# Second-layer scores of a two-layer transformer kernel as three float32r products, with keys and queries split one period ahead

## The reference, cut to what matters

```python
qkv = (h @ Wqkv.T).reshape(b, n, 3, H, HD)
q = _ln(qkv[:, :, 0].transpose(0, 2, 1, 3), qn_g, qn_b)
k = _ln(qkv[:, :, 1].transpose(0, 2, 1, 3), kn_g, kn_b)
v = qkv[:, :, 2].transpose(0, 2, 1, 3)
scores = jnp.einsum('bhnd,bhmd->bhnm', q, k) / jnp.sqrt(jnp.float32(HD))
attn = jax.nn.softmax(scores, axis=-1)
o = jnp.einsum('bhnm,bhmd->bhnd', attn, v)
x = x + o.transpose(0, 2, 1, 3).reshape(b, n, H * HD) @ Wout.T
```

## Time and profile before

| | us |
|---|---|
| runs of the kernel before | 390.44, 391.27, 391.53 (median 391.27) |
| the profiled execution, its own time | 391.85 |
| its span in the trace | 390.1 |
| granted TensorE clock, mean over the span | 0.959 of 2.4 GHz |

### The profile page before, as it was taken

How to read it: one execution, slowest core, us unless ns; L and a number is a source line. 1 busy time by engine, 2 the same in 40 slices (tenths; PEclk the granted TensorE clock), 3 DMA queues, 4 the chain that set the end, 5 groups by cost and what they waited for, 6 DMA issues and landing times.

```text
span 390.1 us, 8940 instructions
## 1 busy us (share of the span) xinstructions
PE 360.2 (92%) x3188; PEld 259.5 (67%) x3188; DVE 258.5 (66%) x608; ACT 267.2 (68%) x660; POOL 151.5 (39%) x158
## 2 busy tenths in 40 slices
PE   7998997769999999999999999999999886799994
PEld 7585676446666666676676676666665564589993
DVE  2856356658767767767767776776777448883425
ACT  3355646688887887887887999888896527347640
POOL 5500233465466466456556546556631011000000
PEclk9999999999999999999999999999999975569999
DMA  4900000002920000000000000000000000000001
GB/s 116 286 7 2 2 2 0 2 0 56 329 104 2 2 3 0 2 3 2 3 0 3 3 2 0 3 1 3 2 0 3 2 2 1 0 2 2 0 3 54
DMA packets 7520, 9.77 MB, mean 25 GB/s; under 512 B 379, under 2 KB 4278, under 8 KB 7478
## 3 DMA queue, kind: packets, MB, share of 16 engines
q1 hardware_dynamic: 5654, 7.11, 5.9%
q10 hardware_dynamic: 1824, 2.10, 1.9%
HBM read 8.68 MB, written 0.52 MB: 24 GB/s over the span
## 4 chain that ended last, share of the span: by engine, by line
PE 82%; DVE 8%; ACT 5%; issue 2%; POOL 1%; DVEq 0%; POOLq 0%; ACTq 0%
PE bank L1356 15%; PE pair L1307 8%; PE pair L1283 7%; PE bank L1307 7%; PE bank L1323 6%; PE bank L1085 6%; PE pair L1323 4%; PE bank L1334 4%; PE bank L1211 2%; PE bank L1501 2%; PE pair L1093 2%; PE pair L1343 2%; PE pair L1219 2%; PE pair L1425 1%; ACT probs L593 1%
## 5 line engine op out<-in xcount | busy, mean ns | idle before, releaser
L423 POOL TENSOR_TENSOR qk_rstd<-qk_ms,minus_half 128x8 f32<-128x8 f32 x32 | 52.5, 1641 | 99.0 <-DVE qk_ms L878 99.0
L1323 PEld LDWEIGHTS bank<-ident,probs 64*128 64x128 f32 x512 | 36.8, 139 | 46.6 <-issue 46.4
L1356 PE MATMUL bank<-probs_T,v_s 128*64 128x256 f32 x512 | 62.3, 385 | 0.6 <-DVE x_att L921 0.6
L890 DVE TENSOR_REDUCE negmax<-pair 128x1 f32<-128x512 f32 x64 | 43.8, 686 | 21.2 <-PE pair L1307 21.2
L602 ACT ACTIVATE probs_T<-bank 128x512 f32<-128x512 f32 x64 | 38.0, 594 | 24.2 <-PE pair L1323 24.0
L593 ACT ACTIVATE probs<-pair,negmax 128x512 f32<-128x512 f32 x64 | 43.9, 687 | 9.3 <-DVE negmax L890 8.3
L1323 PE MATMUL bank<-ident,probs 64*128 64x64 f32 x512 | 43.4, 225 | 2.2 <-DVE probs_T L898 1.3
L1356 PEld LDWEIGHTS bank<-probs_T,v_s 128*64 128x64 f32 x512 | 34.1, 136 | 16.5 <-issue 0.8
L1323 PE MATMUL pair<-ident,probs 64*128 64x64 f32 x512 | 45.1, 228 | 0.0
L898 DVE COPY probs_T<-pair 128x512 f32<-128x512 f32 x64 | 43.7, 683 | 1.1 <-PE pair L1323 1.1
L593 ACT ACTIVATE probs<-bank,negmax 128x512 f32<-128x512 f32 x64 | 43.6, 694 | 0.1
(11 more groups left out here) (252 smaller groups left out, 762.4 us busy)
## 6 DMA issues: line engine op xcount, KB each, us to landing
fc_raw<-in_L_cond_fc2s_dram SPq DMA_DIRECT2D x1, 2048.0 KB, 14.9
x_in<-in_x_dram ACTq DMA_DIRECT2D x1, 512.0 KB, 4.0
w<-in_L_cond_mlp_w_dram SPq DMA_DIRECT2D x2, 256.0 KB, 5.2
wout<-in_L_cond_Wout_dram SPq DMA_DIRECT2D x1, 512.0 KB
b_all<-in_L_cond_b2s_dram SPq DMA_DIRECT2D x1, 512.0 KB, 11.6
out_dram<-final SPq DMA_DIRECT2D x2, 256.0 KB, 2.3
film<-in_L_cond_film_w_dram SPq DMA_DIRECT2D x2, 128.0 KB, 4.3
wq<-in_L_cond_q_w_dram SPq DMA_DIRECT2D x1, 64.0 KB, 2.6
```

What stands on the lines that cost most here:

```text
L423: pool.tensor_tensor(qk_rstd[:, p % 2, :, :].rearrange("p c t -> p (c t)"), qk_ms[:, p % 2, :, :].rearrange("p c t -> p (c t)"), minus_hal ...
L890: dve.tensor_reduce(negmax[:, t % 2, h:h + 1], bank[2 * (t % 2) + h][:, :], AX, ALU.max, negate=True)\
L1323: last = pe.transpose(bank[(4, 6)[q]][:, n * HD:n * HD + HD], probs[rows, t % 2, n // NC, n % NC * P:n % NC * P + P], ident[rows, rows])
L1356: last = pe.matmul(bank[5][h * HD:h * HD + HD, 0:2 * P], v_s[:, m % 4, k, h * HD:h * HD + HD], probs_T[:, r % 2, h, k, :], start=(k == 0), ...
```

## The change

It takes the scores from one float32 product per head to three float32r products (high x high, high x low, low x high), each for both heads in turn. Keys and queries of a piece are now written by `piece_affine` to `kq_full` in float32; a new `keys_high` on VectorE rounds them to `kq_hi`, and a new `keys_low` on GpSimd subtracts to get `kq_lo`. All stages from `project` to `piece_affine` are moved one period ahead: projections at r+6, squares and sums at r+5, norms, turns and affines at r+4. So one more piece is made before the loop; there piece 3's norm goes from GpSimd to VectorE and piece 4's square to ScalarE. A smaller `tn_sq` makes room, for which one wait is added behind the loop.

```diff
-        keys_T = loop("keys_T", [P, 2, N])
-        queries_T = loop("queries_T", [P, 2, N])
+        kq_full = loop("kq_full", [P, 2, 2, 2 * P])
+        kq_hi = loop("kq_hi", [P, 2, 2, N], F32R)
+        kq_lo = loop("kq_lo", [P, 2, 2, N], F32R)
-        tn_sq = tokens("tn_sq", [P, TC, D])
+        tn_sq = tokens("tn_sq", [P, NC, D])
...
+            def keys_low(p):
+                m, half = p // 2, p % 2 * 2 * P
+                pool.wait_ge(kq_high, p + 1)
+                pool.tensor_tensor(kq_lo[:, m % 2, :, half:half + 2 * P], kq_full[:, p % 2, :, :],
+                                   kq_hi[:, m % 2, :, half:half + 2 * P].bitcast(F32), ALU.subtract)\
+                    .then_inc(kq_low, 1)
             norm_scale(2, 1, EPS1)
+            keys_low(0)
             piece_scale(2)
+            keys_low(1)
             piece_scale(3)
+            keys_low(2)
+            piece_scale(4)
             for r in range(HALVES):
                 spread_recip(r)
+                if r + 4 < HALVES:
+                    piece_norm(r + 4)
                 if r + 3 < HALVES:
-                    piece_norm(r + 3)
-                if r + 4 < HALVES:
-                    piece_square(r + 4)
-                    piece_scale(r + 4)
+                    keys_low(r + 3)
+                if r + 5 < HALVES:
+                    piece_square(r + 5)
+                    piece_scale(r + 5)
...
             def piece_affine(p):
-                m, half = p // 2, p % 2 * 2 * P
                 act.wait_ge(kqT_done, p + 1)
-                wait(act, scores_done, 8 * m - 8)
-                act.activation(keys_T[:, m % 2, half:half + 2 * P], turned(p)[:, 0:2 * P], ACT.Identity,
+                wait(act, kq_low, p - 1)
+                act.activation(kq_full[:, p % 2, 0, :], turned(p)[:, 0:2 * P], ACT.Identity,
...
             exponential(0, 0)
             exponential(0, 1)
+            piece_square(4)
             piece_raw(4)
             piece_affine(2)
             exponential(1, 0)
             exponential(1, 1)
+            piece_raw(5)
+            piece_affine(3)
             for r in range(HALVES):
...
-                if r + 3 < HALVES:
-                    piece_affine(r + 3)
-                if r + 5 < HALVES:
-                    piece_raw(r + 5)
+                if r + 4 < HALVES:
+                    piece_affine(r + 4)
+                if r + 6 < HALVES:
+                    piece_raw(r + 6)
...
+            act.wait_ge(tn_ss, NC)
...
+            def keys_high(p):
+                m, half = p // 2, p % 2 * 2 * P
+                dve.wait_ge(kq_affine, p + 1)
+                wait(dve, scores_done, 8 * m - 8)
+                dve.tensor_copy(kq_hi[:, m % 2, :, half:half + 2 * P], kq_full[:, p % 2, :, :]).then_inc(kq_high, 1)
             scaled(2, 1, xn)
+            keys_high(0)
             into_h(2)
             piece_norm(2)
+            keys_high(1)
             maximum(0, 0)
             maximum(0, 1)
             piece_ss(3)
             maximum(1, 0)
             maximum(1, 1)
+            piece_norm(3)
+            keys_high(2)
+            piece_ss(4)
             for r in range(HALVES):
...
                 if 2 * r + 2 < STEPS:
                     maximum(2 * r + 2, 0)
+                if r + 3 < HALVES:
+                    keys_high(r + 3)
                 copy_probs(2 * r)
...
-                if r + 4 < HALVES:
-                    piece_ss(r + 4)
+                if r + 5 < HALVES:
+                    piece_ss(r + 5)
...
             def turn_piece(p):
...
-                if p >= 3:
-                    pe.wait_ge(copied_act, 2 * (p - 3) + 2)
-                elif p == 2:
-                    pe.wait_ge(kq_affine, 1)
+                if p >= 4:
+                    pe.wait_ge(copied_act, 2 * (p - 4) + 2)
+                elif p >= 2:
+                    pe.wait_ge(kq_affine, (1, 3)[p - 2])
             def scores(t):
...
                 if c == 0:
-                    pe.wait_ge(kq_affine, 2 * i + 2)
-                for h in range(2):
-                    rows = slice(h * HD, h * HD + HD)
-                    pe.matmul(bank[2 * (t % 2) + h][:, :], queries_T[rows, i % 2, c * P:c * P + P],
-                              keys_T[rows, i % 2, :], start=True, stop=True).then_inc(scores_done, 1)
+                    pe.wait_ge(kq_high, 2 * i + 2)
+                for n, (queries, keys) in enumerate(((kq_hi, kq_hi), (kq_hi, kq_lo), (kq_lo, kq_hi))):
+                    if c == 0 and n == 1:
+                        pe.wait_ge(kq_low, 2 * i + 2)
+                    for h in range(2):
+                        rows = slice(h * HD, h * HD + HD)
+                        last = pe.matmul(bank[2 * (t % 2) + h][:, :], queries[rows, i % 2, 1, c * P:c * P + P],
+                                         keys[rows, i % 2, 0, :], start=(n == 0), stop=(n == 2))
+                        if n == 2:
+                            last.then_inc(scores_done, 1)
             def turn_probs(t):
...
-                    pe.wait_ge(kq_affine, min(r + 3, HALVES))
-                    pe.wait_ge(v_placed, min(r + 5, HALVES))
+                    pe.wait_ge(kq_affine, min(r + 4, HALVES))
+                    pe.wait_ge(v_placed, min(r + 6, HALVES))
...
             turn_piece(2)
+            project(5)
+            turn_piece(3)
             for r in range(HALVES):
...
-                if r + 3 < HALVES:
-                    turn_piece(r + 3)
+                if r + 4 < HALVES:
+                    turn_piece(r + 4)
                 turn_recip(r)
-                if r + 5 < HALVES:
-                    project(r + 5)
+                if r + 6 < HALVES:
+                    project(r + 6)
```

More of the change, by code:

```diff
@@ L243, in film_attention_then_expert_choice @@
                              "normed"))
-        kqT_done, kq_affine = sem("kqT_done"), sem("kq_affine")
+        kqT_done, kq_affine, kq_high, kq_low = (sem(n) for n in ("kqT_done", "kq_affine", "kq_high", "kq_low"))
         o_rec_done, rec_spread, recT_done, recT_copied, oT_scaled, out_done, out_added = (
@@ L579, in piece_affine @@
             def piece_affine(p):
-                m, half = p // 2, p % 2 * 2 * P
                 act.wait_ge(kqT_done, p + 1)
-                wait(act, scores_done, 8 * m - 8)
-                act.activation(keys_T[:, m % 2, half:half + 2 * P], turned(p)[:, 0:2 * P], ACT.Identity,
+                wait(act, kq_low, p - 1)
+                act.activation(kq_full[:, p % 2, 0, :], turned(p)[:, 0:2 * P], ACT.Identity,
                                bias=col("keys_b"), scale=col("keys_g"))
-                act.activation(queries_T[:, m % 2, half:half + 2 * P], turned(p)[:, 2 * P:4 * P], ACT.Identity,
+                act.activation(kq_full[:, p % 2, 1, :], turned(p)[:, 2 * P:4 * P], ACT.Identity,
                                bias=col("queries_b"), scale=col("queries_g")).then_inc(kq_affine, 1)
@@ L612, in token_means @@
                 for t in tokens:
-                    act.activation(tn_sq[:, t, :], x_att[:, t, :], ACT.Identity, scale=-1.0 / D,
+                    act.activation(tn_sq[:, t % NC, :], x_att[:, t, :], ACT.Identity, scale=-1.0 / D,
                                    accum_out=centre[:, t:t + 1]).then_inc(tn_means, 1)
@@ L618, in token_squares @@
                     act.wait_ge(tn_means, t + 1)
-                    act.activation(tn_sq[:, t, :], x_att[:, t, :], ACT.Square, bias=centre[:, t:t + 1],
+                    act.activation(tn_sq[:, t % NC, :], x_att[:, t, :], ACT.Square, bias=centre[:, t:t + 1],
                                    accum_out=sumsq[:, t:t + 1]).then_inc(tn_ss, 1)
```

## The result

The changed kernel takes 412.31 us (median of 4 runs, 411.95 to 414.83) against 391.4 us of the kernel before on the same chip: 1.055 times as long, with a 95% interval of 1.0515 to 1.0592, or +20.9 us. The profiled execution took 412.5 us, 20.65 more than the profiled one of before. The forecast was 417.

The account below looks back on a forecast made before the run. The prediction took ScalarE's rec_T and VectorE's probs_T copy, not the score matmuls, to bound the kernel. Loop +20.3, entry +5.7 and last periods -0.6 made +25.4 on 391.85, forecast 417 us, range 400 to 423.

Parts of the forecast that it names:

- The bound: Loop's probability transposes: first wait for ScalarE's rec_T, second for VectorE's probs_T copy; score matmuls little or not on the path.
- Part 1: Score matmuls: a step takes 0.92 us, 0.21 less; 13.7 us of TensorE work saved, only -0.6 us of time.
- the rival of 1.56: Score matmuls: float32r heads run one after another, 1.56 us per step, about 421 us; chance 0.10.
- Part 2, the hold: VectorE's loop: keys_high, ahead of copy_probs(2r), is held until GpSimd's qk_n ends; +0.75 us per period.
- the unheld case: VectorE's loop: GpSimd doesn't hold keys_high, +0.14 us per period, about 401; chance 0.20 together with a slow-copy variant.
- Part 2, how often: Loop periods r = 1 to 27: keys_high meets qk_n in all 27, 27 x 0.75 = 20.3 us.
- the collision comes again in each period: Loop: qk_n starts by qk_ms, which comes after mix, so its meeting with keys_high does not drift away.
- The end of the loop loses a projection ... 0: Loop's end: one projection fewer, but second transposes still wait for GpSimd's chain, so the effect is 0.
- part 4: Entry: one more piece before the loop; first exponential about 78.4, first transposes 85.5, second period 92.9: +5.7 us.
- Part 3: GpSimd's loop: keys_low takes 1.28 us, covered by 3.2 us idle before qk_rstd, so it costs nothing.
- The last three periods: Loop's last three periods, where no projection feeds ScalarE: shorter scores give 0.2 us each, -0.6 us.
- Sum: Whole kernel: 20.3 for the hold, 5.7 for the entry, -0.6 for the last periods, together +25.4 us.

Follow-up runs that it names:

- experiment 3: Kernel after with only the high x high product of the scores, both low-part products left out, all waits kept: 394.08 us, 1.0069 times the kernel before.
- experiment 5: Kernel before with scores as three float32r products of the same rounded tensors, no split, no moved piece: 390.68 us, 0.9979 times the kernel before.
- experiment 2: Kernel after with piece_norm(r+4), hence qk_n, ahead of spread_recip(r) in GpSimd's loop: 402.57 us, 1.027 times the kernel before.
- experiment 4: Kernel before plus one unused VectorE rounding copy of 128x512 per period between maximum(2r+2, 0) and copy_probs(2r): 411.43 us, 1.051 times the kernel before.
- experiment 1: Kernel after with keys_high(r+3) moved ahead of maximum(2r+2, 0) in VectorE's loop: 392.93 us, 1.0038 times the kernel before.
- e9: Kernel after with keys_high before the maximum, reciprocal transposes in bank 0, copy_recip before piece_raw, entry reordered, piece 4's square on GpSimd before keys_low(2): 391.08 us, 1.0002.
- e8: Kernel before with the reciprocals' transposes in bank 0 and copy_recip before piece_raw: 391.97 us, 1.0019 times the kernel before.

## Why the prediction was right

- **The bound (right).** The weight load of the first transposes still starts 0.12 us behind rec_T's end (231.05 to 231.17) and that of the second 0.12 behind the copy's (233.46 to 233.58), for the 0.11 read in the earlier trace rows. A page that gave TensorE 92% did not say that cheaper matmuls help. Experiments 3 and 5 show it: 0.43 us less of streams per step changes no period from r = 2 to 27, and the products alone bring 0.8 us.
- **Part 1 (right).** 0.92 us forecast for a step's six float32r matmuls, 0.97 measured: the second pair follows the first at 0.34 and not at 0.21. The heads run side by side; the rival of 1.56 is out.
- **Part 2, the hold (right in mechanism and size).** Forecast: arrival 0.60 behind A, end 0.27 behind qk_n, second transposes at A + 2.38, period 8.18. Measured: 0.65, 0.29, 2.41, 8.18. The step from two other operations in the earlier trace rows to a rounding copy was right. Experiment 2 shows that qk_n's end sets it, experiment 4 that it needs nothing else of the change, and r = 24 that the same place costs 0.17 when qk_n is late (0.14 forecast for the unheld case). The Trainium skill (SBUF — State Buffer, "Who interferes with whom") says that VectorE's two-port copies and casts and GpSimd's instructions exclude each other. The trace agrees for qk_n, rec_wide and qk_sq (1.01 against 0.42 us beside qk_n), but not for GpSimd's powers on 4 and 8 elements a partition, inside which the cast took its plain 0.42.
- **Part 2, how often (wrong).** The sum had 27 x 0.75 = 20.3 for the periods r = 1 to 27. Measured are 23 periods held by qk_n. The 22 from r = 2 to 23 bring +17.0 (0.77 each), r = 1 only +0.15, and r = 24 to 27 together +0.17 where the sum had 3.0. One step that failed is "the collision comes again in each period": it comes again only while all neighbours stand as in the period I had read. At r = 1 the entry's distances still hold, at r = 24 GpSimd does token_scale first and qk_n comes 1.26 us behind keys_high, and at r = 25 and 27 it is behind it as well (+0.17, +0.19, +0.17). token_scale stood in the kernel's text; I had read one period and multiplied it. The other is "The end of the loop loses a projection ... 0" in part 4: r = 26 is held, and still its period is 7.06 against 7.42 before, 1.1 below the other held ones, since the last projection now stands at r = 25. Before, the period falls from 7.42 to 6.37 where the projections end.
- **Part 3 (right).** keys_low costs 1.27 us a period, qk_rstd still has 2.34 us of idle time before it (1.99 in experiment 2, where the order differs), and in the loop nobody waits for keys_low.
- **Part 4 (the entry right by 0.35 us, partly by luck).** First exponential at 79.00 (forecast 78.4), A of r = 0 at 85.71 (85.5), of r = 1 at 92.54 (92.9): +5.35 for 5.7. The first exponential comes 0.6 later than forecast, the way from it to A is 0.4 shorter and the first period 0.6 shorter (6.83 for 7.43), and these cancel.
- **The last three periods (right).** Forecast -0.6; measured -0.66 (r = 28 to 30).
- **Behind the loop (not in the sum).** 83.37 us from A of r = 31 to the end, against 84.98, with the same work. In the profiled execution of before TensorE's granted clock is at its lower level from 316.9 to 347.6 us (30.7 us), in that of the kernel after from 339.8 to 367.1 (27.3 us). Experiment 4, which keeps the float32 scores, has the short one too (27.3) and 83.40 us, so neither the split nor the new products are needed for the -1.6; why the lower level lasts longer in one execution stays open.
- **Sum.** 25.4 forecast, 20.65 measured. Of the 4.75 between them, 3.05 come from the loop (16.65 for 20.3 - 0.6: 0.6 at r = 1, 1.7 at r = 24, 25 and 27, 1.1 at r = 26, less the 0.5 by which r = 2 to 23 cost more), 0.35 from the entry and 1.6 from the stretch behind the loop, less the 0.25 by which the executions differ more than the spans.

That the change loses by the hold is shown (experiments 1, 2 and 4, and r = 24 of the kernel after). What is then left, +1.5 us, is a balance: the entry's +5.8 in the timeline less the shorter periods and the stretch behind the loop (experiment 1). That the entry's order can be bettered is only partly shown: e9 is 1.9 us below experiment 1, by the entry (A of r = 1 at 91.44 for 92.99) and by 0.1 per period together.

## What to carry to other kernels

Before an instruction is put in front of another, look at what GpSimd is doing at that moment, not only at the instruction's own 0.42 us: here one place earlier in the same queue was worth 19.4 us, and GpSimd was busy there too, with an operation that didn't hold the copy. And when a price is found in one period, count in the program the periods where the neighbours stand differently before multiplying. Read behind which record's end TensorE starts: a busy share of 92% hid that 10 us of its work could go and bring 0.8.

## What the runs showed of the hardware

**Between the rounding copy and GpSimd's operations on 128x256 and 128x512 the hold works both ways, and whoever starts first wins.** When qk_n or rec_wide is running, the rounding copy ends 0.28 or 0.29 us behind its end (after, experiments 2, 3 and 4). When the copy is 0.14 us ahead of qk_n, qk_n takes 1.22 instead of 1.04 (experiment 3); rec_wide goes from 0.61 to 0.80 (experiment 2) and qk_sq from 1.04 to 1.22 (experiment 4) in the same way. The VectorE operations that read the scores' and the transposes' banks keep 0.68 (0.66 to 0.69 in the kernel after) beside all of them.

**GpSimd's power doesn't hold the copy, though it started first.** In experiment 1 28 copies start inside qk_rstd and take 0.42; qk_rstd takes 1.79 instead of 1.64 and ends 0.04 behind the copy. At r = 24 after, the copy runs inside the power of 1.06 us, which again ends 0.04 behind it.

**float32r pairs on 64 rows overlap.** In the kernel after, the two heads' matmuls of 512 columns start within 0.04 us of each other. In a step of the loop the records of the first pair take 0.47 to 0.50 us, the others 0.39; the second pair follows the first at 0.31 to 0.34, the third the second at 0.23.

**A slow stretch of TensorE in the entry.** The windows from 78 to 84 us (length, then busy time and count of PE, PEld, DVE, ACT and POOL, then the granted clock), before, after and in experiment 1:

```profile
78.00:84.00 6.00, 3.23 (x41) 1.64 (x38) 4.06 (x8) 5.19 (x14) 3.63 (x4) 1.00 0.00 0
```

```profile
78.00:84.00 6.00, 4.80 (x26) 3.29 (x24) 5.09 (x10) 5.00 (x14) 2.41 (x2) 0.80 0.01 3
```

```profile
78.00:84.00 6.00, 4.64 (x19) 3.41 (x18) 5.10 (x10) 4.95 (x13) 2.43 (x2) 0.52 0.01 3
```

TensorE works part of this stretch at its lower level of 1.2 GHz: from 77.0 to 80.4 us in the kernel after and from 78.3 to 85.1 in experiment 1. Ahead of it TensorE had waited 2.23 us for kq_hi and 0.84 for kq_lo in the kernel after. These waits are not the whole reason: experiment 5 has no split and no such waits, and has the lower level from 79.7 to 86.5. The runs with float32 scores (before, experiment 4, e8) have none there, the nine with float32r scores all have; what brings it stays open. By how much it lengthens the change's entry was not measured by itself. Where it fell into a period of the loop, the period was longer: 9.44 for 8.02 us in experiment 5, and at r = 1 9.00 in experiment 3 for 7.39 in experiment 1.
